# A four-layer graph network on one Trainium2 core: how the adjacency blocks are stored for reuse

## What is computed

```python
x = _layernorm(x + L0(x))   # attention over the incoming edges, 4 heads
x = _layernorm(x + L1(x))   # relu((x + segment_sum(x[src], dst)) @ W)
x = _layernorm(x + L2(x))   # gated messages, mean, two-layer update, its own layer norm
x = _layernorm(x + L3(x))   # mean of (x[src] + rel_emb[type]) @ W_msg.T + b, plus x @ W_self.T
```

## Time and profile before

| | |
|---|---|
| median of 3 runs | 1109.5 us (1106.86 to 1116.73) |
| span of the profiled execution | 1106.8 us |
| TensorE busy | 1011.4 us, 91% |
| VectorE busy | 908.4 us, 82% |
| ScalarE busy | 721.2 us, 65% |
| GpSimd busy | 219.2 us, 20% |
| granted TensorE clock, mean | 0.972 |

### The profile page before, as it was taken

One profiled execution on the slowest core, in us unless ns is written; L12 is line 12 of the kernel. 1 busy time (PEld: TensorE's weight loads), 2 busy tenths in 40 slices (PEclk: granted clock), 3 DMA queues, 4 the chain that ended last, 5 costly groups with the idle time before them and its releaser, 6 DMA issues.

```text
span 1106.8 us, 28220 instructions
## 1 busy us (share of the span) xinstructions
PE 1011.4 (91%) x10463; PEld 867.9 (78%) x10463; DVE 908.4 (82%) x2226; ACT 721.2 (65%) x1559; POOL 219.2 (20%) x260
## 2 busy tenths in 40 slices
PE   3797979699999999995999989779999999999997
PEld 3343557599999999994777777669999999986775
DVE  6775999988998989987988899878787887766754
ACT  3466765555545555547899889677677677776554
POOL 4402240000000000000000000217666667620000
PEclk9899998899999999996999999899999999999998
DMA  6000020345544444412333333234444444457463
GB/s 156 1 1 1 4 67 3 110 144 153 160 137 156 145 155 157 143 46 77 104 125 125 125 112 120 86 110 141 138 135 129 130 139 128 121 185 233 149 169 115
DMA packets 79198, 128.27 MB, mean 116 GB/s; under 512 B 11147, under 2 KB 53206, under 8 KB 78828
## 3 DMA queue, kind: packets, MB, share of 16 engines
q1 hardware_dynamic: 73577, 115.20, 33.5%
q0 software_dynamic: 5056, 10.36, 3.8%
q10 hardware_dynamic: 426, 0.85, 0.3%
HBM read 101.50 MB, written 24.88 MB: 114 GB/s over the span
## 4 chain that ended last, share of the span: by engine, by line
PE 78%; DVE 11%; ACT 5%; issue 3%; DMA 3%; POOL 0%; POOLq 0%; SPq 0%; DVEq 0%; ACTq 0%
PE PS L2416 14%; PE PS L2610 14%; PE PS L2404 11%; PE PS L2593 7%; PE PS L2521 5%; PE PS L2696 5%; PE PS L2489 3%; PE PS L2496 2%; PE PS L2242 2%; PE PS L2255 2%; PE PS L2319 2%; DMA adj_d<-ring 2%; DVE vo L1584 1%; DVE ring L1580 1%; ACT X L1152 1%
## 5 line engine op out<-in xcount | busy, mean ns | idle before, releaser
L1076 ACT CAST vo<-XT 128x768 f32<-128x768 bf16 (+1 forms) x218 | 180.3, 827 | 136.7 <-PE PS L2610 64.1
L912 POOL DMA_INDIRECT XT<-tab,ring x158 | 162.9, 1031 | 109.2 <-PE PS L2610 57.7
L2416 PE MATMUL PS<-vo 128*128 128x133 f32 x1300 | 175.9, 284 | 1.1 <-DVE vo L1686 1.1
L2416 PEld LDWEIGHTS PS<-vo 128*128 128x128 f32 x1300 | 157.2, 191 | 1.2 <-issue 1.2
L2404 PE MATMUL PS<-kp,ring 128*128 128x132 bf16 x1950 | 146.1, 220 | 3.3 <-DVE ring L1554 1.8
L2610 PE MATMUL PS<-vo 128*128 128x128 f32 x984 | 132.8, 279 | 0.0
L2404 PEld LDWEIGHTS PS<-kp,ring 128*128 128x128 bf16 x1950 | 125.3, 97 | 5.5 <-DVE ring L1554 1.9
L1213 ACT CAST ring<-PS 128x512 bf16<-128x512 f32 (+1 forms) x175 | 121.3, 705 | 9.8 <-DMA adj_d<-ring 9.8
L1210 ACT CAST adjf_r<-PS 128x512 fp32r<-128x512 f32 (+1 forms) x175 | 120.3, 698 | 3.6 <-PE PS L2489 3.6
L2610 PEld LDWEIGHTS PS<-vo 128*128 128x128 f32 x984 | 118.9, 191 | 3.0 <-issue 2.4
L1562 DVE TENSOR_TENSOR XT<-iotab,XT 128x768 bf16<-128x768 bf16 (+1 forms) x218 | 119.7, 549 | 1.1 <-ACT XT L1069 1.1
(11 more groups left out here) (345 smaller groups left out, 2167.9 us busy)
## 6 DMA issues: line engine op xcount, KB each, us to landing
ring<-rows_d SPq DMA_DIRECT2D x146, 416.0 KB, 4.6
adj_d<-ring SPq DMA_DIRECT2D x100, 128.0 KB, 1.8
adj_d<-ring SPq DMA_DIRECT2D x75, 96.0 KB, 1.7
ring<-adj_d SPq DMA_DIRECT2D x11, 640.0 KB, 4.8
vo<-adj_d SPq DMA_DIRECT2D x9, 640.0 KB, 4.9
vo<-adj_d SPq DMA_DIRECT2D x8, 480.0 KB, 3.9
ring<-adj_d SPq DMA_DIRECT2D x7, 480.0 KB, 4.3
XT<-tab,ring POOLq DMA_INDIRECT x158
```

Source lines behind the costliest of these rows:

```text
L912: G.indirect_dma_start(far_rows[:, f % FBUF, :], None, tab[2], bass.IndirectOffsetOnAxis(ap=far_row[:, t:t + 1], axis=0)).then_inc(far_in[ ...
L1076: C.copy(ohd[:, k % 3, 0:n, :], ohb[:, k % 3, 0:n, :]).then_inc(hots_wide, 1)
L2416: T.matmul(bank(6 + b % 2)[:, 0:VW], ohd[:, k % 3, i, :], vals[:, k % 3, i, :], start=j == 0, stop=j == JN - 1).then_inc(scattered, 1)
```

## The change

ScalarE copies each piece once, as four-byte values, into a ring of seven (`adj1`), with `ABUF` 7 in place of 6. TensorE multiplies from that ring. The two-byte ring `adj` and its copy are gone, and so is the semaphore `adj_cp`; `build(s)` waits for the one copy of step s - 3. GpSimd, not SyncE, stores the piece to DRAM: its DMA reads four-byte values and writes two-byte ones, so the DMA converts. ScalarE's copy of step s waits until the matmul of step s - 7 is done and the store of step s - 7 has landed. The semaphores `far_in` (now seven) count these landings, and the gathers of L2 count on from there. SyncE keeps the store of the edge-type counts. L3's ring of 4 becomes the last four buffers of the new ring, and `crel` and `crelT` move to other addresses in the same memory.

```diff
-ABUF = 6
+ABUF = 7
@@ memory
-        adj = ring[:, 6400:6400 + ABUF * 4 * P].rearrange("p (r n) -> p r n", r=ABUF)
-        adjf = adjf_r[:, :].rearrange("p (r n) -> p r n", r=XBUF)
+        adj1 = adjf_r[:, :].rearrange("p (r n) -> p r n", r=ABUF)
+        adjf = adj1[:, ABUF - XBUF:ABUF, :]
@@ SyncE
             for q in range(BANKS):
                 w = even_width(q)
-                for b in range(NB):
-                    s = q * NB + b
-                    sp.wait_ge(adj_cp, s + 1)
-                    sp.dma_start(adj_d[q][:, b, 0:w], adj[:, s % ABUF, 0:w]).then_inc(adj_io[s % ABUF], 16)
                 sp.wait_ge(crel_cp, q + 1)
...
             for r in range(ABUF):
-                sp.wait_ge(adj_io[r], adj_stored(r))
+                sp.wait_ge(far_in[r], adj_stored(r))
@@ GpSimd, ahead of the row numbers
+            for q in range(BANKS):
+                w = even_width(q)
+                for b in range(NB):
+                    s = q * NB + b
+                    pool.wait_ge(adjf_cp, s + 1)
+                    G.dma_start(adj_d[q][:, b, 0:w], adj1[:, s % ABUF, 0:w].bitcast(fp32)).then_inc(far_in[s % ABUF], 16)
@@ ScalarE
                     act.wait_ge(adj_mm, s + 1)
-                    if s >= XBUF:
-                        act.wait_ge(applied, s - XBUF + 1)
-                    C.copy(adjf[:, s % XBUF, 0:w], bank(s % 3)[:, 0:w]).then_inc(adjf_cp, 1)
                     if s >= ABUF:
-                        act.wait_ge(adj_io[s % ABUF], 16 * (s // ABUF))
-                    C.copy(adj[:, s % ABUF, 0:w], bank(s % 3)[:, 0:w]).then_inc(adj_cp, 1)
+                        act.wait_ge(applied, s - ABUF + 1)
+                        act.wait_ge(far_in[s % ABUF], 16 * (s // ABUF))
+                    C.copy(adj1[:, s % ABUF, 0:w], bank(s % 3)[:, 0:w]).then_inc(adjf_cp, 1)
@@ TensorE
                 if s >= 3:
-                    pe.wait_ge(adj_cp, s - 2)
+                    pe.wait_ge(adjf_cp, s - 2)
...
-                    o = T.matmul(to[:, 0:w], xs[:, b, :], adjf[:, s % XBUF, 0:w], ...)
+                    o = T.matmul(to[:, 0:w], xs[:, b, :], adj1[:, s % ABUF, 0:w], ...)
```

More of the change, by code:

```diff
@@ L219, in gnn_kernel @@
             shape_only("kp_pad", 4950 - 3200 - P)
-            shape_only("ring_pad", 6272)
-            adjf_r = shape_only("adjf_r", 512 * XBUF)
+            shape_only("ring_pad", 8320 - 512 * ABUF)
+            adjf_r = shape_only("adjf_r", 512 * ABUF)
             xl3_r = shape_only("xl3_r", 3200)
@@ L285, in gnn_kernel @@
         ohx = ring[:, 3840:3840 + 2 * (2 * OH1 + CT)].rearrange("p (r n) -> p r n", r=2)
-        adj = ring[:, 6400:6400 + ABUF * 4 * P].rearrange("p (r n) -> p r n", r=ABUF)
-        adjf = adjf_r[:, :].rearrange("p (r n) -> p r n", r=XBUF)
+        adj1 = adjf_r[:, :].rearrange("p (r n) -> p r n", r=ABUF)
+        adjf = adj1[:, ABUF - XBUF:ABUF, :]
         identr = identr_r[:, :]
-        crel = ring[:, 9472:9472 + 4 * 4 * P].bitcast(fp32).rearrange("p (r n) -> p r n", r=2)
-        crelT = ring[:, 11520:11520 + 4 * CT].bitcast(fp32).rearrange("p (r n) -> p r n", r=2)
+        crel = ring[:, 6400:6400 + 4 * 4 * P].bitcast(fp32).rearrange("p (r n) -> p r n", r=2)
+        crelT = ring[:, 8448:8448 + 4 * CT].bitcast(fp32).rearrange("p (r n) -> p r n", r=2)
         adj3 = ring[:, 0:3 * ACH * 4 * P].rearrange("p (r k n) -> p r k n", r=3, k=ACH)
@@ L535, in gnn_kernel @@
         rel_mm = sem("rel_mm")
-        adj_cp = sem("adj_cp")
         adjf_cp = sem("adjf_cp")
         identr_ready = sem("identr_ready")
-        adj_io = [sem(f"adj_io{n}") for n in range(ABUF)]
+        adj_io = [sem(f"adj_io{n}") for n in range(CBUF)]
         applied = sem("applied")
@@ L563, in gnn_kernel @@
         far_step = sem("far_step")
-        far_in = [sem(f"far_in{n}") for n in range(FSEM)]
+        far_in = [sem(f"far_in{n}") for n in range(ABUF)]
         far_ready = sem("far_ready")
@@ L651, in to_widen @@
             n = chunk_of(s)
-            eng.wait_ge(adj_io[n % CBUF], adj_stored(n % CBUF) + 16 * (n // CBUF + 1))
+            eng.wait_ge(adj_io[n % CBUF], 16 * (n // CBUF + 1))
             eng.wait_ge(applied, NB * BANKS + max(0, s - XBUF + 1))
@@ L910, in _ @@
                 if f >= FSEM:
-                    pool.wait_ge(far_in[f % FSEM], 16 * (f // FSEM))
+                    pool.wait_ge(far_in[f % FSEM], adj_stored(f % FSEM) + 16 * (f // FSEM))
                 G.indirect_dma_start(far_rows[:, f % FBUF, :], None, tab[2],
@@ L1239, in far_scaled @@
                     f = far_at[t]
-                    act.wait_ge(far_in[f % FSEM], 16 * (f // FSEM + 1))
+                    act.wait_ge(far_in[f % FSEM], adj_stored(f % FSEM) + 16 * (f // FSEM + 1))
                     v = far_rows[:, f % FBUF, :]
@@ L2520, in apply1 @@
                 for part, xs in enumerate((XH, XL)):
-                    o = T.matmul(to[:, 0:w], xs[:, b, :], adjf[:, s % XBUF, 0:w], start=b == 0 and part == 0, stop=False, skip_group_check=True)
+                    o = T.matmul(to[:, 0:w], xs[:, b, :], adj1[:, s % ABUF, 0:w], start=b == 0 and part == 0, stop=False, skip_group_check=True)
                 o.then_inc(applied, 1)
```

## The result

The changed kernel takes 1097.68 us (median of 4 runs, 1097.27 to 1098.17), the kernel before on the same chip 1109.34 (1106.86 to 1116.73). The ratio is 0.9892, with an interval of 0.9863 to 0.9921: 1.1% faster. The forecast of 1136 us was wrong: the kernel became faster, not slower. The time lies just inside the range of 1096 to 1162, at its fast end. What came true is the first rival, to which I had given a chance of 0.15 and for which the sum gave 1097.

The account below looks back on a forecast made before the run. TensorE was taken to pace the layer, with ScalarE close behind and stalls at the seams. GpSimd's 1.25 us stores would end the layer 29 us later, hiding the 10 us seam gain: 1106.8 + 29 = 1136 us, range 1096 to 1162.

Parts of the forecast that it names:

- the first rival: GpSimd keeps up in the adjacency layer, at most 0.84 us a store; only the seam gain counts: 1097 us, chance 0.15.
- part 3: GpSimd issues the layer's 175 stores at a gather's price, 1.25 us each, and becomes the new bound.
- Part 1: One ScalarE copy per step instead of two: nothing in the steady part, 0 to 1 us in the first six steps.
- Part 2: Stores leave SyncE's queue, so TensorE's 9.5 us of waits, mostly at group seams, go; about 10 us with the first steps.
- TensorE itself: What limits the layer once the seam stalls go: 173.6 us, of which 173.45 are matmuls now.
- Behind the layer: Row numbers and edge-row loads wait behind the last store; covered with over 30 us to spare, otherwise 4 us.
- The sum's method: First store's start plus 167 store intervals, 2.9 us landing and 1.0 us to the matmul gives the layer's end, 730.2 us.
- The second rival: Gain and loss cancel in the layer at 0.84 to 1.14 us a store: 1100 to 1118 us, chance 0.27.
- The third rival: A store costs over 1.4 us, by slow converting transfer or issues stretched by other work; 1195 us at 1.6, chance 0.13.
- three times the 0.40: The layer's converting transfer decides once a block takes the DMA queues over 1.25 us, against 0.40 us of a step now.
- Room for twice that: Each store reads twice the bytes; the layer's DMA share of 0.40 leaves room for twice that.
- A loss of clock adds little: In the layer TensorE would idle a fifth of each step, and slower steps at lower clock fill that idle time first.

Follow-up runs that it names:

- x8: The changed kernel with each block stored by two DMAs, rows 0 to 63 and 64 to 127: 1110.67 us, ratio 1.0009.
- x7: The changed kernel with each block stored by two DMAs of 128 rows, split by columns: 1113.60 us, ratio 1.0046.
- x14: The changed kernel with each L2 gather replaced by GpSimd's plain load of 128 consecutive rows, so wrong rows are summed: 1096.81 us, one run.
- x13: The changed kernel with L2's gathers fetching 64 rows each instead of 128: 1096.3 us, one run.
- x11: The kernel before, SyncE storing edge-type counts only after the next group's fifth store, and the 1.6 MB broadcast moved behind the layer: 1097.37 us.
- x1: The kernel before, with SyncE storing a group's edge-type counts only after the fifth store of the next group: 1100.20 us, ratio 0.9905.
- x2: The kernel before, both copies and ring of six kept, but GpSimd stores the two-byte blocks unconverted: 1100.74 us, ratio 0.9910.
- x6: The changed kernel with a GpSimd memset behind every store but the last, making 1.19 us a store: 1130.97 us, ratio 1.0190.
- x3: The changed kernel, with GpSimd waiting for ScalarE's copy of the edge-type counts after each group's stores: 1110.02 us, ratio 1.0006.
- x4: The changed kernel with a ring of six in place of seven, 1097.02 us, and with a ring of five, 1103.09 us.
- x0: The changed kernel itself, measured once more: 1096.11 us, ratio 0.9872.

## Why the prediction was wrong

**The step that failed** is the price of a store in part 3, "If a store costs GpSimd what a gather costs", taken at 1.25 us. It measures 0.53. The text did bound it from below by SyncE's 0.59, and that row was the better one. I chose the gather for being on the same engine with the same number of rows. x8 shows that the number of rows does not matter, x7 that the bytes do not, and x14 that being indirect does: with the pause that comes with it, that is 0.7 of the 1.24 us. The prediction's objection to the first rival, that the list "would have to be a third" of the cost, was no objection: what the indirect form adds is more than half (by x13 it does not grow with the list, though). At 0.53 us a store GpSimd has slack in every step, and the sum from the first store to store 167 has no place.

DMA: Bandwidth & Descriptors, Anatomy of one DMA, in the Trainium skill, calls descriptor generation "small, variable" and puts most of the fixed cost of about 2 us into completion; the prediction had held the gathers against it. For the stores the trace agrees: 0.53 us of the 2.6 to landing are issue. A gather's 0.94 us is the dear exception.

**Right once that term is replaced.** Part 1: one copy less gives nothing in the steady part. x11, with two copies, has a layer of 172.54 against 171.90, so one copy less, the converting store and the larger ring together are worth some 0.6 us there, and nothing that the medians show. Part 2: the seams give back their stall. The forecast was 10 us with the first steps, 27.1 us for a wide group and 21.1 for a narrow one; measured are 10.4, 27.30 and 21.50. By x1 and x2 8.5 of it is the wait in SyncE's queue, and most of the other 1.9 the seventh step. That the sum came to 10 was in part luck: the 1.7 us of waiting for the first copy, which it counted as going, stayed, and the 1.5 us of the seventh step, where it had allowed 0 to 1, took their place. The cause of that step was not in the prediction: the earlier trace rows show its wait, but I had not asked what was queued ahead of the store. "TensorE itself" is what is late next. Behind the layer: covered, 406.6 us in both.

**The sum's method** holds where GpSimd is the bound in every step: in x6 it is 3 us short, 2.0 of them GpSimd's pause before store 113. At 1.05 us a block (x7, x8) it is 9 and 6 us short, for the most part because TensorE is slower than that in the wide groups.

**The second rival** was the case of 0.84 to 1.14 us a store. Two stores a block come to 1.05 us; x8 costs the same as the kernel before, 1110.67 us, within its 1100 to 1118, and x7 1113.60, also inside. Its reasoning, that the wide groups stay TensorE's and the narrow ones become GpSimd's, is what their stores show.

**The third rival** was wrong about issues: beside the layer's VectorE work the stores take 531 ns at least and at the median, 745 at most. SBUF — State Buffer, Who interferes with whom, in the Trainium skill, says that a two-port mode of VectorE keeps GpSimd's descriptor writing out, and that tensor_tensor has no such mode. The trace agrees in 174 of the 175 stores, none of them above 560 ns; the one of 745 ns is the layer's first. The rival was nearer the mark about the transfer: "three times the 0.40" was the point from which it decides, and the converting store took it to a little over twice (0.87). "Room for twice that" was all there was.

**"A loss of clock adds little"** held for the case that it was said of, but not for its reason. At the lower granted clock a narrow step took 1.31 us (x3, x6) instead of 0.78, which does not fit in 1.25. In x6 the clock fell too (0.94 over the layer), but GpSimd never waited for it: all but 0.3 us of what the formula lacks is ahead of its store of step 167. In x3, where GpSimd is not the bound, the same loss costs 4.9 us.

**Left open:** the pause of 2.85 us before store 113. With stores of 128 rows it goes by their count and not by time: x7, with two stores a block, has one of 2.14 us before its own store 113, which is in step 56, and shorter ones before stores 215 and 317, 102 apart. Nor is it tied to conversion or ring size (x2, x4). In x8, whose stores have 64 rows instead of 128, there is none before store 113 and one of 1.52 us before store 128, though the copy that it needs is done. What GpSimd does there no view shows. Also open is what makes TensorE's clock fall behind one stall and not behind another. The ring's part in step 6 was not told from that of the lighter ScalarE.

## What to carry to other kernels

An issue row of an indirect DMA is no price for a direct one on the same engine: look first for any direct row, even another engine's. Before pricing a change that moves transfers to another queue, ask what their present queue waits for: here nearly all of the gain was a wait for something else standing ahead of them, and a reordering of a few lines in the old queue, with one broadcast moved, gave the same time as the whole change. A converting DMA cost the engine that issues it nothing here and the DMA engines about double, and the first store of a burst of seven landed late.

## What the runs showed of the hardware

- GpSimd is held 0.53 us by a direct DMA, whether it stores or loads, converts or not, and for 64 or 128 rows, half or full columns (after, x2, x7, x8, x14: 528 to 539 ns at the median). A gather holds it for 0.94 us (0.90 for 64 rows), with 0.30 us before the next.
- Converting four bytes to two in a store raised the DMA share from 0.41 to 0.87 (wide) and from 0.40 to 0.94 (narrow) at the same GB/s. The median landing is 2.6 us after the issue, in x2 2.0; the first of a burst of seven released its waiter after 4.6.
- In x3 TensorE's waits for the copy rose by 11.3 us (13.0 less the 1.7 that the changed kernel has too) and the layer by 17.1. Of the rest 4.9 us are steps at the lower clock (0.51 in 688 to 695 us), behind idle times of 1.66, 1.48 and 3.10 us in the narrow groups. Behind 2.52 us in a wide group the clock stayed at 1.00.
- GpSimd pauses 2.85 us before store 113, counted from 0, whatever the time and the ring (changed kernel, x0, x2, x4); 2.14 us in x7. With stores of 64 rows (x8) the pause is 1.52 us and comes before store 128.
